# A residual stream kept in expert order: token rows scattered once, no padding, output rows scattered at the end

## The chip, the cores and the metric

The kernel runs on one core of a Trainium2 chip. The metric is the device time of one execution in microseconds (us). A core has TensorE (PE, matrix products), VectorE (DVE), ScalarE (ACT), GpSimd (POOL) and SyncE (SP), each with its own instruction stream. They order themselves by semaphores. SyncE and GpSimd issue DMA transfers; indirect ones (a row address per partition, from a table) come from GpSimd.

## The reference

One decoder layer on x of 4 x 512 tokens with 512 features (2048 tokens, 16 tiles of 128 rows):

```python
x = x + attn(_layernorm(x))                          # linear attention, 16 heads of 32
x = x + experts(_layernorm(x), itok, ctx, ctx, ctx)  # expert of a token: from its token id
x = x + ffn(_layernorm(x))                           # ternary weights, 512 -> 2048 -> 512

# attn:    q = elu(x Wqk + bqk) by heads, v = silu(x Wv + bv), u = silu(x Wu + bu)
#          out = q (k^T v) per head; out = layernorm(out) * ln_g + ln_b
#          return (u * out) @ Wo + bo
# experts: e = min(token_id // 6250, 3); g = silu(x ctx[e]^T); u = x ctx[e]^T
#          return (g * u) @ ctx[e]^T           (512 x 512 per expert, 4 experts)
# ffn:     w -> clip(round(w / scale), -1, 1) * scale, scale = mean(|w|)
#          return (silu(x wu^T) * (x wg^T)) @ wd^T
```

The drawn token ids spread over the four experts, so the number of tokens of an expert is not a multiple of 128.

## The kernel before

[...] 

**Attention**, four batches of four tiles. `batch(b, first, last)` exists on each engine. PE makes q (four products of 12 matmuls), v, the output projection of the batch before (`project`), key transposes, u (four products), the key-value sums (L1230) and the head products (L1244). The head norm and the projection of batch b - 1 are done inside batch b, and those of the last batch behind the loop: filler matmuls (`keep_busy`), `head_norm`, `project`, then VectorE's `last_sum` and `last_norm`. A normalised tile (n2) is scattered by GpSimd (`scatter`, L328) into the DRAM tensor `sorted_tokens`, at row positions in which each expert begins at a multiple of 128; before, ten SyncE stores fill this tensor with zeros, for the padding rows. Positions are made on VectorE in `routing_starts` and `routing_positions`, at the end of the first batch.

**Experts**, 19 tiles (16 + 3 for padding; `SLOTS`). For a tile: SyncE loads it (`sorted_tile`), PE transposes it (`xs_transpose`), ACT and DVE make a high and a low half in float16 (`xsT`), PE makes z, ACT and DVE make z * silu(z) (h_mul), PE transposes that, and `second(i - 1)` is the product of the tile before. The weights are picked by a register that PE reads (`tile_expert`). VectorE copies the result (`y_copy`), GpSimd stores it to `sorted_outputs`.

**Ternary units.** The three weight matrices of the last stage come in 12 units of 1 MB. VectorE makes two sign passes (`signs_of`), PE transposes them (`unit_transposes`, 32 matmuls), ACT copies (`unit_copies`). Before, four units are ahead of the expert tiles (the fourth behind the first transpose), five in steps 0 to 3, three behind the last tile, followed by 96 filler matmuls.

**Last stage.** Four batches, 16 chunks each of two 8-matmul groups (up, gate; L1350) and eight down matmuls (L1360). For its first batch, GpSimd gathers four tiles from `sorted_outputs` back into token order, VectorE sums, makes statistics and norms, PE transposes and ACT and DVE split. For later batches one tile is gathered, summed and normalised every four chunks, and turned by a DMA transpose (`x3_turned`). `finish` adds the residual, and SyncE stores the output tiles (`stored`).

## Time and profile before

| | before |
|---|---|
| median of 3 runs | 757.99 us (757.53 to 758.48) |
| profiled execution, its own time | 756.31 us |
| its span | 754.7 us |
| PE busy | 726.2 us, 96% |
| VectorE, ScalarE, GpSimd busy | 388.9, 275.9, 108.6 us |
| mean granted clock of PE | 0.989 of full speed |
| memory traffic | 47.73 MB read, 18.61 MB written |

The span is the time from the first to the last record of the profile; the own time is what a timer around the execution shows. PE's busy time counts overlapping instructions once. [...] Positions in a row are us from the start of the span.

### The profile page before, as it was taken

How to read it: one execution, taken by the hardware profiler on the slowest of the kernel's cores; microseconds unless marked ns; L12 is line 12 of the kernel's file. 1: busy time of each engine (PE TensorE's matmuls, PEld its weight loads, DVE VectorE, ACT ScalarE, POOL GpSimd, SP SyncE). 2: the span in 40 equal slices, each digit the busy share in tenths (PEclk: the TensorE clock that was granted, in tenths of full speed). 3: DMA queues.
4: the chain of work that ended last, by engine and by line, in shares of the span. 5: the costliest groups of instructions: out<-in, count | busy, mean ns of one | idle time of the engine just before them, and what ended most of it. 6: DMA issues, size and time to landing. Idle time of an engine off the chain costs nothing.

```text
span 754.7 us, 12300 instructions
## 1 busy us (share of the span) xinstructions
PE 726.2 (96%) x4136; PEld 391.0 (52%) x4137; DVE 388.9 (52%) x672; ACT 275.9 (37%) x430; POOL 108.6 (14%) x154
## 2 busy tenths in 40 slices
PE   7999999999997889999997999999999999999997
PEld 5565556556556666555546444444444444444443
DVE  5678666666636955444457433454434534443223
ACT  4365554554554355222324222222223222222221
POOL 4203034034021400000004100000000000000000
PEclk9999999999999999999999899999999999999999
DMA  8983034034044396222212011121101210020001
GB/s 238 391 322 137 1 128 151 0 127 152 1 159 176 113 361 231 79 85 96 83 42 71 28 29 28 28 80 33 24 19 28 83 28 14 14 70 0 0 0 57
DMA packets 45168, 69.93 MB, mean 93 GB/s; under 512 B 19024, under 2 KB 19024, under 8 KB 44112
## 3 DMA queue, kind: packets, MB, share of 16 engines
q1 hardware_dynamic: 41136, 56.38, 22.4%
q0 software_dynamic: 4000, 13.11, 5.0%
q8 instruction: 21, 0.34, 0.2%
q14 instruction: 11, 0.09, 0.0%
HBM read 47.73 MB, written 18.61 MB: 88 GB/s over the span
## 4 chain that ended last, share of the span: by engine, by line
PE 85%; DVE 4%; DMA 3%; issue 2%; ACT 2%; POOL 2%; SPq 1%; DVEq 0%; POOLq 0%; ACTq 0%
PE bank L1079 31%; PE bank L1350 30%; PE bank L1360 14%; PE bank L1072 5%; PE bank L1230 2%; PE bank L1244 1%; DMA nrm<-in_L_ffn_W_down_dram 1%; PE bank L1265 1%; DMA stage<-in_L_attn_Wv_dram 1%; POOL rs L320 1%; DVE st L589 1%; DMA sorted_tokens<-n,pos_now 1%; SPq L184 1%; DMA n<-sorted_outputs,pos_now 0%; DVE region L774 0%
## 5 line engine op out<-in xcount | busy, mean ns | idle before, releaser
L1350 PE MATMUL bank<-w_att,region 128*128 128x512 f16 (+1 forms) x1024 | 233.4, 381 | 0.8 <-ACT w_att L550 0.8
L1350 PEld LDWEIGHTS bank<-w_att,region 128*128 (+1 forms) x1024 | 100.6, 98 | 123.3 <-issue 3.9
L1045 DVE SCALAR_TENSOR_TENSOR tmp<-tmp,hk,bank 128x512 f32<-128x512 f32 x64 | 47.8, 747 | 150.2 <-PE bank L1350 149.8
L1360 PE MATMUL bank<-region,tmpA 128*128 (+1 forms) x504 | 119.1, 379 | 0.0
L1079 PE MATMUL bank<-w_moe,tmpA 128*128 x456 | 104.9, 380 | 1.5 <-DVE tmpA L934 1.5
L1079 PE MATMUL bank<-xT,w_att 128*128 128x512 f16 x384 | 86.6, 381 | 1.6 <-DVE region L774 1.6
L564 ACT ACTIVATE tmp<-bank,qs 128x512 f32<-128x512 f32 x64 | 44.0, 687 | 119.5 <-PE bank L1350 119.5
L568 ACT ACTIVATE tmpA<-tmp 128x512 f16<-128x512 f32 x64 | 40.3, 630 | 122.0 <-DVE tmp L1045 122.0
L1360 PEld LDWEIGHTS bank<-region,tmpA 128*128 128x128 f16 x504 | 49.2, 98 | 59.6 <-DVE stage L1028 0.9
L1079 PEld LDWEIGHTS bank<-w_moe,tmpA 128*128 128x128 f16 x456 | 44.5, 98 | 47.2 <-issue 2.0
L1048 DVE TENSOR_TENSOR tmpA<-tmp,tmpA 128x512 f16<-128x512 f32 x64 | 44.3, 693 | 45.6 <-ACT tmpA L568 45.6
L318 POOL TENSOR_SCALAR ve<-mv 128x1 f32<-128x1 f32 (+1 forms) x37 | 10.2, 275 | 381.1 <-DVE mv L1008 204.6
L1079 PEld LDWEIGHTS bank<-xT,w_att 128*128 128x128 f16 x384 | 37.3, 98 | 44.4 <-DVE region L774 2.4
L1079 PE MATMUL bank<-w_att,region 128*128 128x512 f16 x192 | 43.0, 383 | 1.0 <-DVE region L727 1.0
L1079 PE MATMUL bank<-w_att,xT 128*128 128x512 f16 x192 | 42.8, 379 | 0.0
L501 ACT ACTIVATE region<-bank 128x512 bf16<-128x512 f32 x48 | 25.3, 603 | 28.9 <-PE bank L1265 24.7
L1079 PEld LDWEIGHTS bank<-w_att,region 128*128 128x128 f16 x192 | 18.6, 98 | 24.2 <-DVE region L727 2.2
L1079 PEld LDWEIGHTS bank<-w_att,xT 128*128 128x128 f16 x192 | 18.7, 98 | 21.3 <-DVE region L731 0.5
L1265 PE MATMUL bank<-ident_b,w_att 128*128 128x128 bf16 x384 | 24.9, 226 | 4.0 <-DVE w_att L864 4.0
L929 DVE TENSOR_TENSOR tmp<-bank,tmp 128x512 f32<-128x512 f32 x19 | 13.1, 690 | 28.7 <-ACT tmp L529 28.7
L1265 PEld LDWEIGHTS bank<-ident_b,w_att 128*128 128x128 bf16 x384 | 23.4, 102 | 6.1 <-DVE w_att L864 4.9
L320 POOL TENSOR_TENSOR rs<-ve,halfs 128x1 f32<-128x1 f32 (+1 forms) x37 | 25.8, 698 | 3.1
(138 smaller groups left out, 769.9 us busy)
## 6 DMA issues: line engine op xcount, KB each, us to landing
stage<-in_L_ffn_W_up_dram SPq DMA_DIRECT2D x8, 1024.0 KB
stage<-in_L_ffn_W_gate_dram SPq DMA_DIRECT2D x8, 1024.0 KB, 5.6
sorted_tokens<-a SPq DMA_DIRECT2D x10, 512.0 KB, 10.7
n<-sorted_tokens SPq DMA_DIRECT2D x20, 256.0 KB, 2.6
stage<-in_ctx_dram SPq DMA_DIRECT2D x4, 1024.0 KB
stage<-in_L_ffn_W_down_dram SPq DMA_DIRECT2D x4, 1024.0 KB
nrm<-in_L_ffn_W_down_dram SPq DMA_DIRECT2D x4, 1024.0 KB, 7.7
out_dram<-stage SPq DMA_DIRECT2D x16, 256.0 KB, 2.1
```

Source lines behind the costliest of these rows:

```text
L320: pool.tensor_tensor(rs[i][:, tiles], ve[i][:, tiles], halfs[:, tiles], ALU.pow).then_inc(s[done], 1)
L501: act.activation(dst, src, ACT.Copy).then_inc(s["unit_copy"], 1)
L564: act.activation(sil, up_ps[:, :], ACT.Silu, scale=qs[:, 0:1]).then_inc(s["up_act"], 1)
L568: act.activation(hid[:, cc % 2, 0], h32, ACT.Copy).then_inc(s["hid_hi"], 1)
L1045: dve.scalar_tensor_tensor(out=h32, in0=sil, scalar=hk[:, 0:1], in1=gate_ps[:, :], op0=ALU.mult, op1=ALU.mult).then_inc(s["hid_mul"], 1)
L1048: dve.tensor_tensor(hid[:, cc % 2, 1], h32, hid[:, cc % 2, 0], ALU.subtract).then_inc(s["hid_lo"], 1)
L1072: mm = pe.transpose(dst[:, i * P:(i + 1) * P], src(i), ident[:, :])
L1079: mm = pe.matmul(dst, lhs(*step), rhs(*step), start=(start and n == 0), stop=(stop and n == len(steps) - 1))
L1230: mm = pe.matmul(kv_ps[:, cut], kk[:, t, cut], vv[:, t, cut], start=(t == 0), stop=(t == T - 1))
L1265: mm = pe.matmul(q_ps[r][:, cut], signs[:, j, h, r, cut], ident_b[:, :], start=(h == 0), stop=(h == 1))
L1350: mm = pe.matmul(dst, w[:, bass.ds(cf_c, 1), k * P:(k + 1) * P].rearrange("p a n -> p (a n)"), x3T[:, bass.ds(b, 1), i, k].rearrange("p a ...
L1360: mm = pe.matmul(ffy_ps[t][:, :], hid[:, parity, i, t * P:(t + 1) * P], tern[2][:, bass.ds(c, 1)].rearrange("p a n -> p (a n)"), start=(st ...
```

## The change

The tokens stay in expert order from the scatter to the output.

- Positions have no padding: expert e begins where e - 1 ends. A tile of 128 sorted rows can hold rows of several experts. 19 steps (`STEPS`) walk through pairs of tile and expert: step i works on tile i - expert, and `routing_steps` makes the tables of expert, tile, address of the tile, and for each step a column `own` that is 1/65536 for rows of the step's expert and 0 for others. VectorE adds y * own into the residual tile (`y_add`, tile by register). No zeros are stored.
- The residual tiles are scattered as well, into `sorted_residual`, by GpSimd (16 transfers), and loaded back in this order by SyncE (four of 1 MB); so are the row numbers, into `sorted_ids` (16 transfers of 128 x 4 bytes), and read back as `row_id`.
- The sorted tiles are transposed once and their halves stay in the buffer of the attention weights (`sorted_T`, the same memory as `x3T`), from which PE's first product reads at a register address. Sign buffers move to `late`, two in place of three, over buffers of the attention stage.
- Ten units stand in steps 0 to 9; none behind the last step. Filler: 70 matmuls behind the first unit; the 50 and the 96 are gone.
- The first four tiles of the last stage are normalised in steps 13 to 18 and turned by DMA; there is no gather. Outputs are scattered by GpSimd to their token rows.
- In the last attention batch the four u products come behind the head products, in the place of the filler.
- Loops over batches (GpSimd) and steps (all engines) are written out.

The diff, cut:

```diff
@@ sync
-                sp.wait_ge(s["zero_src"], 1)
-                with sp.Fori(0, (SLOTS + 1) // 2) as i:
-                    sp.dma_start(xs_v[:, bass.ds(2 * i, 2)], a32[:, :, :]).then_inc(s["zeroed"], 16)
...
+        sp.wait_ge(s["scattered"], 16 * NT)
+        for i in range(3):
+            sorted_tile(i)
         sp.wait_ge(s["sign_b"], 1)
         unit(1, 0)
...
+        sp.wait_ge(s["x1_sent"], 16 * NT)
+        sorted_residual(0)
+        sp.wait_ge(s["sign_b"], 2)
+        unit(1, 1)
+        sp.wait_ge(s["sign_b"], 3)
+        unit(1, 2)
+        for n in range(6):
+            sp.wait_ge(s["tx_mm"], n + 1)
+            sorted_tile(n + 3)
+            if n % 2 == 0:
+                sorted_residual(1 + n // 2)
+            sp.wait_ge(s["sign_b"], n + 4)
+            unit(2 + n // 3, n % 3)
@@ gpsimd
+        def scatter_residual(b):
+            for n in range(T * b, T * b + T):
+                pool.indirect_dma_start(x1_dram, row_of(n), resid[:, n], None).then_inc(s["x1_sent"], 16)
+
+        def scatter_ids(b):
+            for n in range(T * b, T * b + T):
+                pool.indirect_dma_start(id_dram, row_of(n), tok_id[:, n:n + 1], None).then_inc(s["id_sent"], 16)
...
+            if 0 < b < B - 1:
+                scatter_residual(b - 1)
+                scatter_ids(b - 1)
...
         for t in range(T):
             rsqrt_tile(1, "o_aggr", T * (B - 1), t, "rs_o_last")
+        scatter_residual(B - 2)
+        scatter_ids(B - 2)
+        scatter_ids(B - 1)
         rsqrt_tile(2, "x2_aggr", T * (B - 1), 0, "rs2_last")
...
         scatter(B - 1, T - 1)
+        pool.memset(halfs[:, :], -0.5).then_inc(s["scatter_out"], 1)
+        scatter_residual(B - 1)
+        def send_out(b):
+            for t in range(T):
+                pool.wait_ge(s["out_made"], T * b + t + 1)
+                pool.indirect_dma_start(out_rows, bass.IndirectOffsetOnAxis(ap=row_id[:, T * b + t:T * b + t + 1], axis=0),
+                                        out_slot[t], None).then_inc(s[f"out_done{t}"], 16)
@@ scalar
+        ctx_hi(B - 1, 3)
+        magnitudes(B - 1, 0)
+        act.wait_ge(s["a_mul"], K * (B - 1))
+        o_copies(B - 1)
+        magnitudes(B - 1, 1)
+        u_act(B - 1, 0)
+        magnitudes(B - 1, 2)
+        u_act(B - 1, 1)
+        u_act(B - 1, 2)
         affine(B - 1, 0)
+        affine(B - 1, 1)
+        gated_hi(B - 1, 0)
+        gated_hi(B - 1, 1)
+        u_act(B - 1, 3)
@@ vector, routing_steps at the end of the first batch (count_of: three comparisons, two sums)
+            count_of(expert, at, [pad_f[:, 1, e:e + 1] for e in range(1, E)])
+            route(dve.scalar_tensor_tensor(out=tile, in0=expert, scalar=-float(P), in1=at, op0=ALU.mult, op1=ALU.add))
+            route(dve.tensor_scalar(row, tile, lane[:, 0:1], None, ALU.add))
+            count_of(of_row, row, [base[:, e:e + 1] for e in range(1, E)])
+            route(dve.tensor_tensor(own[:, :], of_row, expert, ALU.is_equal))
+            route(dve.tensor_scalar(own[:, :], own[:, :], CTX_SCALE ** -2, None, ALU.mult))
@@ vector, the steps
+        dve.wait_ge(s["scatter_out"], 1)
         signs_of(0, 1)
...
-            dve.tensor_scalar(ys_slot[slot], y_ps[:, :], CTX_SCALE ** -2, None, ALU.mult).then_inc(s["y_evac"], 1)
+            dve.scalar_tensor_tensor(out=x_tile(tile), in0=y_ps[:, :], scalar=own[:, i:i + 1], in1=x_tile(tile),
+                                     op0=ALU.mult, op1=ALU.add).then_inc(s["y_evac"], 1)
...
+        def expert_step(i):
+            if i == 0:
+                signs_of(0, 2)
+            elif i < 10:
+                signs_of(1 + (i - 1) // 3, (i - 1) % 3)
             dve.wait_ge(s["z_act"], i + 1)
             dve.wait_ge(s["h_hi"], i)
             dve.tensor_tensor(h32, z_ps[:, :], sil, ALU.mult).then_inc(s["h_mul"], 1)
+            if i + 1 < NT:
+                xs_lo(i + 1)
+            if 15 <= i:
+                x3_lo(i - 15)
+            if i > 0:
+                y_add(i - 1)
+            if 14 <= i < 14 + T:
+                x3_normalise(i - 14)
             dve.wait_ge(s["h_hi"], i + 1)
             dve.tensor_tensor(hT[:, 1], th_ps[:, :], hT[:, 0], ALU.subtract).then_inc(s["h_lo"], 1)
+            if 13 <= i < 13 + T:
+                if i == 13:
+                    dve.wait_ge(s["y_evac"], i)
+                x3_stats(i - 13)
@@ tensor
-        keep_busy(kv_ps, 50)
+        u_part(B - 1, 0, False)
+        u_part(B - 1, 1, False)
+        u_part(B - 1, 2, False)
+        head_norm(B - 1, True, (0, 1))
+        u_part(B - 1, 3, False)
+        head_norm(B - 1, True, (2, 3))
...
+        def first(i):
+            w = weights_of(i)
+            off = pe.value_load(step_off[0:1, i:i + 1], min_val=0, max_val=(B - 1) * 2 * K * S + S - P)
+            pe.wait_ge(s["xs_lo"], min(i, NT - 1) + 1)
+            pe.wait_ge(s["h_mul"], i)
+            product(z_ps[:, :], lambda i, j, k: sorted_T[:, bass.ds(off + (i * K + k) * S, P)], w).then_inc(s["z_mm"], 1)
...
-        keep_busy(ps[3], 96)
...
         pe.wait_ge(s["unit_copy"], 12 * T)
+        pe.wait_ge(s["y_evac"], STEPS)
+        pe.wait_ge(s["x3_in"], 16 * T)
```

How the change moves instructions, at three places. In these rows a name is an engine's tile: bank is a PSUM bank, region holds q, k, v, u and the gated rows, late the transposed inputs and later the signs, ones the filler's operand.

On PE, behind the last batch's key transposes, there stood before:

```order
L1079 MATMUL bank<-xT,w_att 128x512 x12
L1072 MATMUL bank<-ident,stage 128x128 x4
L1079 MATMUL bank<-xT,w_att 128x512 x36
L1230 MATMUL bank<-region 128x128 x16
L1244 MATMUL bank<-kvm,region 128x128 x16
L1086 MATMUL bank<-ones 128x128 x50
L1282 MATMUL bank<-abssum,ones 128x3
L1072 MATMUL bank<-ident,region 128x128 x16
L1079 MATMUL bank<-w_att,region 128x512 x48
```

and now:

```order
L1063 MATMUL bank<-ident,stage 128x128 x4
L1227 MATMUL bank<-region 128x128 x16
L1241 MATMUL bank<-late,region 128x128 x16
L1070 MATMUL bank<-late,w_att 128x512 x36
L1063 MATMUL bank<-ident,region 128x128 x8
L1070 MATMUL bank<-late,w_att 128x512 x12
L1063 MATMUL bank<-ident,region 128x128 x8
L1285 MATMUL bank<-abssum,ones 128x3
L1070 MATMUL bank<-w_att,region 128x512 x48
```

The four u products (48 matmuls) moved from ahead of the key-value sums to behind the head products, around the head transposes.

On GpSimd, from the last four rsqrts of the head norm to the last scatter, now (before, the two rows with sorted_residual and sorted_ids were not there):

```order
L309 TENSOR_SCALAR ve<-mv 128x1
L311 TENSOR_TENSOR rs<-ve,halfs 128x1
L326 DMA sorted_residual<-resid,pos 2048x512 x4
L330 DMA sorted_ids<-tok_id,pos 2048x1 x8
L309 TENSOR_SCALAR ve<-mv 128x1
L311 TENSOR_TENSOR rs<-ve,halfs 128x1
L309 TENSOR_SCALAR ve<-mv 128x1
L311 TENSOR_TENSOR rs<-ve,halfs 128x1
L322 DMA sorted_tokens<-n,pos 2048x512
```

Twelve indirect transfers moved in between the last head rsqrt and the first rsqrt of the last normalisation.

On PE, from the last expert product to the last stage, before:

```order
L1079 MATMUL bank<-w_moe,tmpA 128x512
L1265 MATMUL bank<-ident_b,w_att 128x128 x96
L1086 MATMUL bank<-ones 128x128 x96
L1072 MATMUL bank<-ident,nrm 128x128 x16
L1350 MATMUL bank<-w_att,region 128x512 x32
```

and now:

```order
L1070 MATMUL bank<-w_moe,tmpA 128x512 x2
L1070 ISA
L1070 MATMUL bank<-w_moe,tmpA 128x512
L1342 MATMUL bank<-w_att,region 128x512 x32
L1352 MATMUL bank<-region,tmpA 128x512 x8
```

Three units, the filler and the four transposes of the first normalised tiles are gone from between them.

## Rows read from the trace of the kernel before

**Rows 1.** The page: busy time and share, and PE in 40 slices.

```profile
PE 726.2 (96%) x4136; PEld 391.0 (52%) x4137; DVE 388.9 (52%) x672; ACT 275.9 (37%) x430; POOL 108.6 (14%) x154
...
PE   7999999999997889999997999999999999999997
```

**Rows 2.** Table by stages: stage, length, PE, PEld, DVE, ACT, POOL busy, clock, DMA.

```profile
225.00:270.00 45.00, 36.88 (x359) 28.36 (x358) 30.97 (x56) 18.39 (x32) 12.97 (x20) 0.93 0.48 176
...
396.00:416.00 20.00, 14.85 (x210) 12.74 (x207) 15.00 (x26) 8.71 (x16) 10.29 (x13) 0.94 0.21 67
```

**Rows 3.** Chain that ended last: start, length, what.

```profile
258.69 4.68 DMA sorted_tokens<-n,pos_now
...
397.00 2.03 DMA sorted_outputs<-n
...
416.06 9.16 PE bank L1350 x32
426.94 3.45 PE bank L1350 x16
```

**Rows 4.** PE's instructions in order: start, length, instruction, count.

```profile
285.33 2.75 PE L1079 MATMUL bank<-w_moe,tmpA 128*128 x12
...
293.18 2.75 PE L1079 MATMUL bank<-w_moe,tmpA 128*128 x12
...
388.36 0.60 PE L1072 MATMUL bank<-ident,n 128*128 128x128 f32 x4
388.80 2.75 PE L1079 MATMUL bank<-w_moe,tmpA 128*128 x12
391.39 0.60 PE L1072 MATMUL bank<-ident,tmp 128*128 128x128 f32 x4
393.49 2.76 PE L1079 MATMUL bank<-w_moe,tmpA 128*128 x12 [1.50 <-DVE tmpA L934]
```

**Rows 5.** PE's instructions, end of attention and start of experts.

```profile
228.85 3.96 PE L1244 MATMUL bank<-kvm,region 128*128 128x128 f32 x32 [0.78 <-DVE kvm L836]
...
244.13 9.38 PE L1079 MATMUL bank<-w_att,region 128*128 128x512 f16 x42 [0.51 <-DVE region L727]
...
269.70 2.98 PE L1079 MATMUL bank<-w_moe,tmpA 128*128 x12
```

**Rows 6.** VectorE's instructions, end of attention.

```profile
236.82 0.55 DVE L597 TENSOR_SCALAR region<-region,mv,rs 128x512 f32<-128x512 f32 x1 [0.76 <-POOL rs L320]
...
247.17 0.68 DVE L750 TENSOR_TENSOR resid<-bank,resid 128x512 f32<-128x512 f32 x1
...
256.52 0.55 DVE L597 TENSOR_SCALAR n<-resid,mv,rs 128x512 f32<-128x512 f32 x1 [0.77 <-POOL rs L320]
```

**Rows 7.** GpSimd's instructions, end of attention.

```profile
223.98 0.96 POOL L328 DMA_INDIRECT sorted_tokens<-n,pos_now  x1 [0.30 <-issue]
...
258.69 2.09 POOL L328 DMA_INDIRECT sorted_tokens<-n,pos_now  x1 [0.30 <-issue]
```

**Rows 8.** The line that reads a tile's expert, 330 to 343 us.

```profile
L1299 PEldq TENSOR_LOAD <-tile_expert x4: 297/300/307, 331.6 to 341.7; - x4
```

**Rows 9.** VectorE's instructions, end of the first batch.

```profile
61.94 0.16 DVE L684 CAST starts<-starts_i 1x19 f32<-1x19 int32 x1
...
63.08 0.16 DVE L691 CAST tile_expert<-te_f 1x19 int32<-1x19 f32 x1
...
68.55 0.70 DVE L772 TENSOR_SCALAR tmp<-tmp 128x512 f32<-128x512 f32 x1 [2.34 <-ACT tmp L441]
```

**Rows 10.** Last issues (start, length), then DMA issues with median us to landing.

```profile
750.11 2.31 SPq L277 DMA_DIRECT2D out_dram<-stage  x4
...
n<-sorted_tokens SPq DMA_DIRECT2D x20, 256.0 KB, 2.6
...
out_dram<-stage SPq DMA_DIRECT2D x16, 256.0 KB, 2.1
...
n<-sorted_outputs,pos_now POOLq DMA_INDIRECT x16, 3.4
```

More of the change, by code:

```diff
@@ L469, in batch @@
                 ctx_hi(b, 0)
+            if last:
+                return
             magnitudes(b, 0)
@@ L824, in batch @@
                 ctx_lo(b, 3)
+                if last:
+                    kv_mask(b)
                 dve.wait_ge(s["rs2"], 2 * b)
@@ L1308, in second @@
             pe.wait_ge(s["y_evac"], i)
-            moe(y_ps[:, :], hT, e).then_inc(s["y_mm"], 1)
-        def tile_step(i, units, slot, slot_count, first):
-            e = expert(i)
-            pe.wait_ge(s["xs_lo"], i + 1)
-            pe.wait_ge(s["h_mul"], i)
-            moe(z_ps[:, :], xsT, e).then_inc(s["z_mm"], 1)
-            xs_transpose(i + 1, slot, slot_count)
-            if not first:
+            product(y_ps[:, :], lambda i, j, k: hT[:, i, k * P:(k + 1) * P], w).then_inc(s["y_mm"], 1)
@@ L1318, in tile_step, with expert_step @@
+        def expert_step(i):
+            first(i)
+            if i + 1 < NT:
+                xs_transpose(i + 1)
+            if i > 0:
                 second(i - 1)
-            for g, j in units:
-                unit_transposes(g, j)
+            if i == 0:
+                unit_transposes(0, 2)
+            elif i < 10:
+                unit_transposes(1 + (i - 1) // 3, (i - 1) % 3)
             pe.wait_ge(s["h_mul"], i + 1)
```

552 lines of the change are left out of this document (239 added, 313 removed).

## The prediction

> **What bounds the kernel now.** I read the page first: TensorE (PE) is busy 96% of the span [rows 1], so time goes away only where PE works without use or waits. Its row of 40 slices is full but for the first and last one, slices 13 to 15 and slice 22, and the table by stages shows two holes: 225 to 270 us holds only 36.9 us of PE work, and 396 to 416 us only 14.9 us [rows 2]. Both counts include matmuls that only keep PE busy. The chain that ended last says what these two places wait for [rows 3]. Before the experts it is the scatter of the last normalised rows, which lands 4.68 us after 258.69. After the experts it is a round trip through memory: a 2.03 us store of the last expert outputs at 397.00, then a gather, sums, statistics, norms and transposes until the last stage starts at 416.06. [...]
>
> The instruction list of PE gives the pace between the two. The first product of one step with a sign unit starts at 285.33, the next one's at 293.18: 7.85 us. A step without a unit is two products of 12 matmuls (2.59 us each, from 388.80 to 391.39) and two groups of transposes (0.44 us each, 388.36 to 388.80), 6.06 us [rows 4]. So a unit costs 7.85 - 6.06 = 1.79 us of PE, and there is no bubble in either kind of step.
>
> **The end of the attention stage.** Before, PE goes through the head products at 228.85, then 50 filler matmuls and the head transposes, and has 42 projection matmuls left at 244.13, which end at 253.5 [rows 5]. Afterwards the four u products (4 x 2.59 = 10.4 us) stand behind the head products and fill what the filler and the waits took. Head products can start about 9.9 us earlier, at 219 (10.4, less some 0.5 for key copies that the u products used to cover); they take 3.9 us. Three u products run to 230.7. The last head norm ended at 237.37 [rows 6], some 8.5 us behind the start of the head products; now four norms of the third batch (1.9 us) and its four scatters are ahead of it on VectorE and GpSimd, so I take 11 us: 230. It is met by PE at 230.7. The rest (transposes, u product 3, transposes: 4.4 us) ends at 235.1. The gating of the last two chunks follows, 3.5 us (half of the 6.8 us between 237.37 and 244.13), and 38 matmuls remain at 216 ns, 8.2 us: the projection ends at 247, not 253.5.
>
> VectorE carries the chain on. Its last norm ended at 257.07, 9.9 us after the first residual sum at 247.17 [rows 6]. From 242 (gating, scales, one pair of sign passes) it would end at 251 to 252. But GpSimd now has 12 indirect transfers (four of residual rows, eight of ids) in its queue ahead of the last rsqrts. One takes 0.96 us and a gap of 0.30 [rows 7], so 12 take 15.1 us; with the start at 229 and a sign pair (2.5 us) in their way, the first rsqrt can start at 247, where it is wanted at 243.7. This takes back about 2.5 us: last norm at 254, last two scatters done at 256, landed at 259, instead of 263.4. The first sorted tile is read next (2.6 us, [rows 10]), turned on PE (0.44 us) and split by ScalarE and VectorE (0.6 and 0.7 us, the times of such passes elsewhere), so the first expert product starts 4.5 us later, at 263.5, instead of 269.70 [rows 5], since the three units that stood before it are now inside the steps or done already. Id transfers are not in the trace. Their bounds are nothing (below) and 2.09 us each (above, the slowest scatter [rows 7]); I take the residual's price, as both have 128 rows. The bounds are then 243.7, no delay, or a first rsqrt at 256, 9 us late.
>
> The slowest scatter started at 258.69, under a pair of sign passes: 2.09 us, against 0.96 [rows 7]. The wait that the change adds ahead of the next sign passes spares the last scatters this, about 1.9 us together, contained in the sum. [...]
>
> **The staircase.** 19 steps before and after, 38 products. Transposes of sorted tiles fall from 19 to 15 in the steps; ten units instead of five stand in them. PE work: 38 x 2.59 + 34 x 0.44 + 10 x 1.79 = 131.3 us, plus the 1.5 us wait ahead of the last product [rows 4]; plus 1.7 us because PE will be nearly idle before it, as it was before the 9.16 us row, where the low clock cost 2.26 us (bounds 0 and 2.3). From 263.5 the last product ends at 398.0. The last stage now waits for the last VectorE sum, 0.75 us: 398.8.
>
> Three things could lengthen steps, and I cost each at nothing. The register work: the reads of the step's expert take 0.30 us each [rows 8], PE's sequencer does them ahead of the array, and now two stand before the first product with four more register instructions. In steps without units they must fit between the end of h_mul (about 1.4 us after a product: a silu and a multiplication of 0.6 to 0.7 us) and 3.03 us; two reads with what follows take 1.0 us. If the cover were gone: 0.5 us x 9 plain steps. VectorE: the sum replaces a copy of the same 0.69 us, norms, statistics and low halves of the first four tiles are four passes more in a 5.6 us step that had four such passes of 0.6 to 0.7 us. DMA: the second and third unit loads stand behind the last residual scatter (landed at about 263) and a 1 MB load; both land by 272, wanted at 280. Turning the first batch by DMA: the last of the four is issued behind step 18's first product, 7 us before PE is through; if it takes what a gather takes, 3.4 us [rows 10], more than 2 us are left. Its upper bound is 2 us past that.
>
> **The last stage** thus starts at 398.8 against 416.06: -17.3. Its slow first matmuls: PE idles only 1.5 and 0.8 us before it now, so I take the 2.26 us as gained: -2.3 (bounds 0 and -2.3). Inside it, a sum, a gather and a position copy per tile go, all hidden under PE; nothing.
>
> **Early cost.** The tables of steps, tiles and lanes are made at the end of the first batch on VectorE. The old tail of seven instructions takes from 61.94 to 63.24 [rows 9], 0.19 us each; 33 take 6.1 us: +4.8 us. Statistics of the heads queue behind it, then the q clip of the next batch, which had waited 2.34 us for ScalarE [rows 9]; PE waits for it. So +2.4 us, all batches later. Residual scatters of batches 0 and 1 on GpSimd (8 transfers, 10.1 us each time) stand behind the last rsqrt that a batch of 56 us waits for, on an engine that is busy 14% of the time [rows 1]: nothing; if they did delay the next rsqrt, 10 us at most. The 10 zeroing stores go, nothing waited for them; nothing.
>
> **The end.** Output tiles leave by SyncE, issue to landing 2.1 us; the last four issues begin at 750.11 and end at 752.42 [rows 10]. Now GpSimd scatters them: four at 1.26 us, so the last is issued at about 754.0 and lands 3.4 us later (the gathers' median [rows 10]): 757.4 against 754.2, +3.2. A scatter may land as the fastest gather would, 2.5 us: +2.3.
>
> **Sum**: -17.3 - 2.3 + 2.4 + 3.2 = -14.0 us against the profiled execution, whose own time is 756.31 with a span of 754.7; so 742.3, and with the median of the runs (757.99, 1.7 above it) 744.0.
>
> **Rivals.**
> (a) GpSimd's queue is late, in the form in which it still ends faster: the twelve transfers cost the upper bound, the experts start 6 us later than I say. 750.0. [...]
> (b) Other side: the same queue decides alone if the twelve take so long that the first rsqrt starts 14 us later than 247, that is (261 - 229)/12 = 2.7 us each. At 3.0 us each it starts at 265, 18 us late, and the time is 762.0, slower. Against it: no transfer in the trace takes that long; for it: ids of 4 bytes are in no row.
> (c) The steps become issue-bound: every matmul of the first product needs two registers. If it took 260 ns, not 216, a step grows by 0.53 us, 10 us in all: 754.0. Against it: the reads of 0.30 us and eight register instructions per product leave no bubble in the steps before [rows 4, 8], so the sequencer is well ahead of the array.
> (d) Nothing is lost on GpSimd: ids are cheap and the clock stays up: 740.0.
> (e) The change doesn't do what it says: the last stage still waits for the turned first tiles. They have 2 us or more to spare; each tile late by more adds that. 747.0 for 3 us more.
>
> **How the numbers follow.** Forecast and its surroundings (741 to 748) 0.52, (d) 0.13, (a) 0.12, (e) 0.08, (c) 0.07, (b) 0.08. Range 738 to 752: it leaves out (b), (c) and the far ends, under 2 in 10. The measurement can tell some 0.2% (1.5 us). Faster needs under 756.5: all but (b) and the worst of (c): 0.90; same 0.03; slower 0.07.
>
> **What would show it.** PE's gap before the last stage under 3 us with no filler; head products near 221 (with the early cost) and experts' first product near 266; steps of 7.85 and 6.06, then 5.6 us; VectorE's tables some 6 us at 62; final landing some 7 us behind the last matmul. It would be wrong if GpSimd's transfers before the last rsqrt took over 25 us together, if steps with units grew past 7.9 us, or if the batches' PE work gained new waits.

## The result, and the profile after

The change makes the kernel slower. In the same session of the chip the kernel after took 765.56 us (median of 4 runs, 763.66 to 766.73) and the kernel before 757.76 us (4 runs, 757.15 to 758.48). The ratio is 1.010, with a 95% interval of 1.0077 to 1.0123. The prediction was 744.0 us, 738 to 752. The profiled execution of the kernel after, the fastest of the four, has an own time of 763.66 us and a span of 761.9 us.

The page of the kernel after: busy time and share, and PE in 40 slices.

```profile
PE 715.7 (94%) x3948; PEld 381.1 (50%) x3978; DVE 386.8 (51%) x655; ACT 273.1 (36%) x426; POOL 131.0 (17%) x171
...
PE   8998999899899869999998999999999999999993
```

PE has 10.5 us less work than in [rows 1] and the span is 7.2 us longer. Slice 22, after the experts, reads 8 instead of 7; the attention batches (slices 4 to 11) now have three slices of 8 where all were full, slice 15 (the switch to the experts) has 6, and in the last slice PE works 3 tenths instead of 7.

The table by stages, of the kernel after, with the columns of [rows 2].

```profile
225.00:270.00 45.00, 39.85 (x308) 26.88 (x305) 29.32 (x62) 21.19 (x32) 29.86 (x37) 1.00 0.49 176
270.00:396.00 126.00, 118.40 (x857) 72.78 (x858) 71.02 (x92) 49.38 (x93) 7.97 (x10) 0.99 0.46 157
396.00:416.00 20.00, 18.50 (x92) 8.99 (x90) 10.97 (x19) 5.45 (x9) 1.57 (x4) 1.00 0.24 46
```

The stage from 396 to 416 us holds 18.50 us of PE work where it held 14.85 [rows 2]: this hole is mended. The stage from 225 to 270 us holds more too (39.85 instead of 36.88), but everything here comes some five us later than before, and a part of the hole now lies behind 270: PE waits there for 5.5 us until 273.78, and the row from 270 to 396 us holds 118.40 us (124.16 before). The chain that ended last shows where the time went instead (start, length, what).

```profile
138.50 5.65 DVE late L759
...
146.19 7.04 PE bank L1070 x24
...
200.07 5.74 DVE late L759
...
207.84 7.04 PE bank L1070 x24
...
417.43 7.07 PE bank L1342 x32
```

One VectorE multiplication (L759, the gating product `gated_mul`) takes 5.65 us in the third batch and 5.74 us in the last one, and PE's next 24 matmuls take 7.04 us where 24 take 5.26 us elsewhere: PE had waited for 3.24 us, and the mean granted clock (the share of PE's full speed that the profile shows) behind the wait is 0.65 for 2.4 us and 0.80 for the next 4.4, a mixture of 0.50, which the trace has from 146.93 to 150.35 us, and 1.00 on both sides of it. The last stage starts at 417.43 instead of 416.06 [rows 3]; its first 32 matmuls take 7.07 us instead of 9.16.

VectorE's instructions (start, length, line, operation) and under them GpSimd's, both in the third batch of the kernel after.

```profile
137.90 0.68 DVE L799 SCALAR_TENSOR_TENSOR w_moe<-bank,w_moe 128x512 f32 x1
138.50 6.24 DVE L759 TENSOR_TENSOR late<-tmpA,region 128x512 f32<-128x512 f32 x2
144.84 0.69 DVE L763 TENSOR_TENSOR region<-late,region 128x512 f16<-128x512 f32 x1
...
128.42 1.08 POOL L326 DMA_INDIRECT sorted_residual<-resid,pos  x1 [0.19 <-issue]
...
137.68 0.96 POOL L330 DMA_INDIRECT sorted_ids<-tok_id,pos  x1 [0.30 <-issue]
138.66 4.92 POOL L335 TENSOR_TENSOR resid<-resid,bo_bc 128x512 f32<-128x512 f32 x4
```

GpSimd's eight transfers fill 128.42 to 138.64, and the four bias adds that used to follow the rsqrt (the reciprocal square root of a norm) at once now start at 138.66, 0.16 us behind the gating product. VectorE's first multiplication then ends only when the four bias adds end (at 144.15 us, they at 143.58). The one reads `tmpA` and `region`, the other `resid` and `bo_bc`.

PE's instructions around it, and at the last product and the last stage.

```profile
140.19 2.75 PE L1070 MATMUL bank<-w_att,late 128*128 128x512 f16 x12
146.19 7.04 PE L1070 MATMUL bank<-w_att,late 128*128 128x512 f16 x24 [3.24 <-DVE region L767]
...
413.67 2.76 PE L1070 MATMUL bank<-w_moe,tmpA 128*128 x12 [1.50 <-DVE tmpA L1002]
417.43 7.07 PE L1342 MATMUL bank<-w_att,region 128*128 128x512 f16 x32 [1.00 <-issue]
```

The end of the program, in GpSimd's instructions, and then the DRAIN instructions that the engines' queues have at the end of the block, of the kernel after (lengths in ns, start us).

```profile
749.63 0.96 POOL L374 DMA_INDIRECT out_dram<-stage,row_id  x1 [73.43 <-DVE stage L1020]
...
753.42 0.96 POOL L374 DMA_INDIRECT out_dram<-stage,row_id  x1 [0.30 <-issue]
...
L1399 DVEq DRAIN  x1: 2218/2218/2218, 749.2 to 749.2; - x1
...
L1399 POOLq DRAIN  x1: 5292/5292/5292, 756.4 to 756.4; - x1
```

The last scatter has landed at 756.4. What follows is not a transfer: it is GpSimd's own closing DRAIN, 5.29 us, to 761.7. In the kernel before the same instruction stood at 647.3, a hundred us ahead of the end:

```profile
L1408 POOLq DRAIN  x1: 4661/4661/4661, 647.3 to 647.3; - x1
```

### The profile page after: what moved, and what is told of

Its sections match the earlier page's. It is cut to its first block, busy times and chain, and to the rows that moved or that the text cites. A ratio compares the mean times of both kernels' runs of the same rounds, so it can differ in the third digit from the quotient of the medians.

```text
span 761.9 us, 11591 instructions
## 1 busy us (share of the span) xinstructions
PE 715.7 (94%) x3948; PEld 381.1 (50%) x3978; DVE 386.8 (51%) x655; ACT 273.1 (36%) x426; POOL 131.0 (17%) x171
## 4 chain that ended last, share of the span: by engine, by line
PE 82%; DVE 6%; POOL 4%; issue 3%; ACT 2%; SPq 1%; DMA 1%; DVEq 0%; ACTq 0%; POOLq 0%
PE bank L1342 29%; PE bank L1070 28%; PE bank L1352 14%; PE bank L1063 4%; PE bank L1263 3%; PE bank L1227 2%; DVE late L759 1%; POOL sorted_ids L330 1%; PE bank L1241 1%; POOL sorted_tokens L322 1%; DMA stage<-in_L_attn_Wv_dram 1%; DVE region L606 1%; POOL sorted_residual L326 1%; SPq L190 1%; DVE st L598 1%
## 5 line engine op out<-in xcount | busy, mean ns | idle before, releaser
L1070 PE MATMUL bank<-late,w_att 128*128 128x512 f16 x384 | 86.1, 379 | 4.0 <-DVE region L806 3.9
L1070 PEld LDWEIGHTS bank<-late,w_att 128*128 128x128 f16 x384 | 37.2, 98 | 46.4 <-DVE region L806 4.7
L1070 PE MATMUL bank<-w_moe,w_att 128*128 x228 | 52.4, 380 | 3.8 <-issue 2.2
L1070 PE MATMUL bank<-w_moe,tmpA 128*128 x228 | 52.3, 379 | 1.5 <-DVE tmpA L1002 1.5
L1070 PE MATMUL bank<-w_att,late 128*128 128x512 f16 x192 | 46.5, 400 | 6.6 <-DVE region L767 6.6
L1070 PEld LDWEIGHTS bank<-w_moe,w_att 128*128 x228 | 22.2, 97 | 28.3 <-issue 6.8
L374 POOL DMA_INDIRECT out_dram<-stage,row_id x16 | 16.2, 1012 | 110.4 <-DVE stage L1020 108.0
L1070 PEld LDWEIGHTS bank<-w_att,late 128*128 128x128 f16 x192 | 19.2, 102 | 31.3 <-DVE region L767 8.1
L1070 PEld LDWEIGHTS bank<-w_moe,tmpA 128*128 128x128 f16 x228 | 22.2, 98 | 25.3 <-issue 2.0
L1263 PE MATMUL bank<-ident_b,late 128*128 128x128 bf16 x384 | 24.8, 225 | 5.5 <-DVE late L903 5.5
```

The lines of the kernel that those rows point to most:

```text
L374: pool.indirect_dma_start(out_rows, bass.IndirectOffsetOnAxis(ap=row_id[:, T * b + t:T * b + t + 1], axis=0), out_slot[t], None).then_inc( ...
L1070: mm = pe.matmul(dst, lhs(*step), rhs(*step), start=(start and n == 0), stop=(stop and n == len(steps) - 1))
L1263: mm = pe.matmul(q_ps[r][:, cut], signs[:, u % 2, h, r, cut], ident_b[:, :], start=(h == 0), stop=(h == 1))
```

## The experiments

Seventeen kernels ran. Ratios are to the kernel before in the same session; its medians there lay between 755.8 and 757.8 us.

**1. The bias adds back in their place.** The changed kernel, with the eight transfers behind the next batch's bias adds instead of ahead of them.

```diff
 def batch(b):
     ... (bias adds of batch b)
+    if b > 1:
+        scatter_residual(b - 2)
+        scatter_ids(b - 2)
     ...
-    if 0 < b < B - 1:
-        scatter_residual(b - 1)
-        scatter_ids(b - 1)
```

> The changed kernel with one thing moved: GpSimd's eight transfers of residual rows and ids of a batch stand behind the four bias adds of the next batch, not ahead of them. Theory A (the bias adds, which read two tiles, now run at the time of VectorE's gating product, which reads two tiles as well, and hold it for 5 us in each of two batches): the 5.65 us gating product returns to 0.7 us, PE's two waits of 3.2 and 3.3 us go, some 10 us less: 755 to 756. Rival (the indirect transfers themselves hold VectorE or the memory): they now run just at the time of the gating product, it stays long, the time stays near 765.

Measured: 757.45 us (10 runs), ratio 1.001 (0.9994 to 1.0026). One edit in GpSimd's order gives back 8.1 us by the medians, 7.1 if each is taken against the kernel before of its own session. VectorE's and GpSimd's rows of this run:

```profile
138.87 1.28 DVE L759 TENSOR_TENSOR late<-tmpA,region 128x512 f32<-128x512 f32 x2
...
128.58 5.55 POOL L335 TENSOR_TENSOR resid<-resid,bo_bc 128x512 f32<-128x512 f32 x4
134.30 1.48 POOL L326 DMA_INDIRECT sorted_residual<-resid,pos  x1 [0.17 <-issue]
```

The two gating products take 1.28 us again instead of 6.24, beside transfers instead of bias adds.

**2. The same collision in the kernel before.** The kernel before, with eight spare transfers at the place where the changed kernel has its own.

```diff
 rsqrt(1, "o_aggr", T * b + T, slice(0, T), "rs_o", b)
+if not first and not last:
+    for n in range(8 * b - 8, 8 * b):
+        pool.indirect_dma_start(more_dram, bass.IndirectOffsetOnAxis(ap=pos[:, n:n + 1], axis=0),
+                                ones[:, :], None).then_inc(s["more_sent"], 16)
 ...
-with pool.Fori(1, B - 1) as b:
+for b in range(1, B - 1):
     batch(b, False, False)
```

The loop over the two middle batches is written out as well, on GpSimd, as it is in the kernel after.

> The kernel before, with eight indirect transfers of 128 rows to a spare DRAM tensor behind the head's rsqrt in each of the two middle batches, at the place where the changed kernel has its residual and id transfers; nothing else of the change. Theory A: the bias adds behind them are delayed by 10 us onto the gating product, which costs 5 us in each of two batches: 768. Rival (the long batches come from something else in the change, the address of the transposed inputs or the written-out loops): 758, no change.

Measured: 767.23 us, ratio 1.0135 (1.0102 to 1.0169): the whole loss and more, without a residual stream that is sorted. The written-out loop alone was not run; the rows show the transfers' part. Here it is another VectorE instruction that is caught, a copy of 4 integers per partition:

```profile
136.43 5.10 DVE L767 COPY pos_now<-pos 128x4 int32 x1
...
136.57 4.92 POOL L336 TENSOR_TENSOR resid<-resid,bo_bc 128x512 f32<-128x512 f32 x4
```

**3. Register reads earlier.** In the changed kernel, the two reads of the next step's expert and offset are made ahead of the unit's 64 weight loads and matmuls, not behind them.

```diff
-def expert_step(i):
-    first(i)
+def expert_step(i, reads):
+    first(i, *reads)
     ...
+    reads = reads_of(i + 1) if i + 1 < STEPS else None
     (unit transposes, then those of h)
+    return reads
```

> The changed kernel with PE's two register reads for the next step's first product placed ahead of the unit transposes, not behind the h transposes. Theory B (in steps with a unit PE's sequencer is no further ahead than the last few matmuls, so the two reads of 0.30 us each with their register work show as the 0.8 us, not 0.44 us, from h transposes to product): unit steps fall from 8.22 to 7.85 us, ten of them, some 3.5 us less: 762. Rival (first products are slow to start because both operands have register addresses): steps stay at 8.22 us, 765.6.

Measured: 761.79 us, ratio 1.0078 (1.0052 to 1.0104): 3.8 us less by the medians, 2.8 against the kernels before of the two sessions; ten steps by 0.37 us make 3.7. PE's rows, first of the kernel after, then of this run:

```profile
300.57 0.61 PE L1063 MATMUL bank<-ident,tmp 128*128 128x128 f32 x4
301.38 2.76 PE L1070 MATMUL bank<-w_moe,w_att 128*128 x12 [0.20 <-issue]
...
309.58 2.76 PE L1070 MATMUL bank<-w_moe,w_att 128*128 x12 [0.19 <-issue]
```

```profile
300.95 0.61 PE L1063 MATMUL bank<-ident,tmp 128*128 128x128 f32 x4
301.40 2.75 PE L1070 MATMUL bank<-w_moe,w_att 128*128 x12
...
309.24 2.75 PE L1070 MATMUL bank<-w_moe,w_att 128*128 x12
```

From the transposes to the product it takes 0.81 us in the one and 0.45 us in the other, from step to step 8.20 and 7.84 us. The gap of 0.37 us is shown as only 0.20 "issue", since the recorded end of the transposes lies 0.16 us behind the start of the next product where nothing is waited for.

**4 and 5. The end of the program.** In run 4 the last four output tiles are stored by SyncE in sorted order, so this kernel leaves out the way back to the token rows for them, and its output is not the reference's; the amount of work is the same. In run 5 the scatters stay, but SyncE waits for their landing instead of GpSimd.

```diff
 send_out(B - 1)
-for t in range(T):
-    pool.wait_ge(s[f"out_done{t}"], 16 * B)
 (SyncE, at its end)
+for t in range(T):
+    sp.wait_ge(s[f"out_done{t}"], 16 * B)
```

> The changed kernel with the last four output tiles stored by SyncE as they lie (the rows of these tiles stay in expert order in the output), so that GpSimd's last transfer is 70 us before the end. Theory C (GpSimd's drain at the end of the program takes 5.3 us, and starts only when its last transfer has landed; before it lay under PE): 7.3 us less, 758.3. Rival (only the transfers are slower, 2.7 against 2.1 us and 1.26 against 0.66 us apart): 2.5 us less, 763.

> The changed kernel, with one edit: SyncE instead of GpSimd waits for the last output scatters to land, so GpSimd's program ends with its last issue (754.38) instead of with the landing (about 756.1), and its final DRAIN can begin some 2 us earlier. Theory: the DRAIN is a fixed piece of some 5.3 us behind GpSimd's last instruction, so the span ends near 759.7 instead of 761.7 and the median is 763.5. Rival: the DRAIN itself waits for the transfers, in which case it begins earlier and is as much longer, and the median stays at 765.5. A DRAIN that costs nothing once its transfers are waited for elsewhere would give 760.

Measured: run 4 757.72 us, ratio 1.002 (1.0003 to 1.0037), 7.8 us less than the kernel after (6.9 by the sessions). Run 5 764.35 us, ratio 1.0089 (1.0063 to 1.0115), too near to 1.010 to tell by time; its trace tells it. The last scatter is over at 757.14 and SyncE knows of its landing at 759.2; GpSimd's DRAIN (recorded from 754.1, 8312 ns) ends at 762.4, 5.3 us behind its last instruction, as it ended 5.3 us behind the wait in the kernel after:

```profile
756.18 0.96 POOL L376 DMA_INDIRECT out_dram<-stage,row_id  x1 [0.30 <-issue]
...
L1399 POOLq DRAIN  x1: 8312/8312/8312, 754.1 to 754.1; - x1
...
L1399 SPq DRAIN  x1: 13/13/13, 759.2 to 759.2; - x1
```

So it is a piece of 5.3 us behind whatever GpSimd does last, in both kernels. From the last scatter's end to the span's end it is now 5.6 us, and was 7.5 (754.38 to 761.9).

**6. Ids later.** The eight id transfers ahead of the last norm moved behind the last residual scatter.

> The changed kernel, with one edit: the eight id transfers of batches 2 and 3 go behind the last residual scatter instead of ahead of the first reciprocal square root of the last norm. The twelve transfers took 244.41 to 261.72, so four take some 5.7 us and end near 250, before the square root is wanted at 258.2. Theory (the queue of twelve costs 2 us or a little more): VectorE's wait of 2.76 at 262.68 shrinks to the 0.8 that the square root takes, the staircase starts 2.0 earlier, median 763.5. Rival (what the front gains is lost again behind it, because the wait for the sorted rows or the clock decides): 765.5.

Measured: 777.62 us, ratio 1.0265 (1.0233 to 1.0298): 12 us worse than the kernel after. The near part came as expected (the pair of sign passes that waits for the scatters starts at 269.31 instead of 271.24), the rest did not. Three loads of 1 MB took 20.7 to 23.7 us to land, where the same three took 9.9 to 13.3 in the kernel after, and PE waited once for 8.04 us:

```profile
308.60 1.12 PE L1063 MATMUL bank<-ident,n 128*128 128x128 f32 x4 [8.04 <-DMA n<-sorted_tokens]
```

**7. Tables later.** The tables of tile, offset and expert made behind the second pair of sign passes, where VectorE idles some 5 us.

> The changed kernel, with one edit: the 28 or so small VectorE operations that make the tables of tile, offset and expert (62.81 to 68.40, 5.6 us) are moved from the end of the first batch to the place behind the second sign pass pair, where VectorE idles 5.4 us for the first sorted tile. Theory (they cost some 2.3 us where they stand: a TensorE wait of 2.38 instead of 0.63 at 72.83 and 0.86 at 79.05): the second batch's products start 2.3 earlier and the median is 763.2. Rival (the time at the front is given back later through the clock, or the new place is on the path to the first expert product): 765.5 to 766.

Measured: 764.96 us, ratio 1.0113 (1.0084 to 1.0142). The key-value sums of the first two batches are 58.97 us apart, not 61.15, and the next two 59.95, not 61.65, but the first product of the experts waits 3.12 us for the tables and runs 5.16 us, at a granted clock of 0.50. VectorE had made the tables by 275.56 us, and only then the low half of the first tile. The rival was right: nothing clear of noise is left at the end.

**8. All of them.** Edits 1, 3, 5, 6 and 7 together.

> The changed kernel with the edits of the bias-add run, the early register reads, the late ids, the late tables and SyncE's final waits together. Theory (the costs are separate and add): 757.5 from the bias-add run, less 3.8 of the register reads, less 2.0 of the ids, less 2.3 of the tables, less 1 to 2 of the end if the DRAIN is a fixed piece: 748, between 746 and 750, faster than the kernel before (756.8) by 1.1 per cent. Rival (the gains overlap, since a shorter middle lets TensorE's clock fall more often or the last stage waits for another engine): 752 or more.

Measured: 761.3 us, ratio 1.0052 (1.0031 to 1.0074). The theory failed by 13 us; the late ids are in it.

**9 to 12. Ids in the second batch.** Positions are known after the first batch, so all sixteen id transfers can be issued in the second one, where GpSimd idles for 30 us. Run 9 does this on top of run 1. Run 10 adds eight spare scatters of 2 KB rows behind the last residual scatter, where run 6 had its ids. Runs 12 and 11 add edits 3 and 5, with the tables early and late.

```diff
 (GpSimd, behind the bias adds of batch b)
+if b == 1:
+    pool.wait_ge(s["rows_made"], 1)
+    for n in range(B):
+        scatter_ids(n)
 if b > 1:
     scatter_residual(b - 2)
```

> The kernel with the bias-add run (757.45), with one more edit: all sixteen id transfers are issued in the second batch, behind GpSimd's bias adds, where GpSimd idles from 78.7 to 108.8 (16 by 1.27 is 20.3 us); none is left in the middle batches or ahead of the last norm. Theory (ids cost only where they stand in the way or run beside the weight loads): the 2.76 us wait for the first reciprocal square root of the last norm falls to 0.8, and nothing is lost elsewhere: 755.4. Rival (an id transfer slows the DMA engines wherever it stands, or the gain is lost at the switch to the experts): 757.5 or more.

> The kernel with early ids, plus eight spare scatters of 2 KB rows (to a tensor that nothing reads) behind the last residual scatters, where the run with late ids had its eight transfers of 4-byte rows. GpSimd's time for them is the same 10 us. Theory (it was the 4-byte rows that slowed the DMA engines there: a 6 us stretch moved 13 GB/s and loads landed in 17 to 24 us instead of 8 to 10): the spare rows add 2 MB, some 5 us of the DMA engines' time, most of it hidden: within 3 us of the kernel with early ids, 755.4 to 758.5. Rival (any eight scatters there hold up the loads or the instruction fetches behind them): 12 us more, 767.

> Bias adds first (757.45), ids early (less 2.0), register reads early (less 3.8), GpSimd's program ending with its last issue (less 2.0), the tables at their first place: 749.7 if the four add, between 748 and 752, faster than the kernel before by 0.9 per cent. Rival (a gain is lost again at the switch to the experts, through the clock or late instructions): 754 or more.

> Bias adds first, ids early, register reads early, GpSimd's program ending with its last issue, and the tables of tile and expert made behind the second sign pass. Theory (the tables' early cost of some 2 us is saved and the new place hides them): 1 to 2 us below the same kernel with the tables at their first place, 748. Rival (the new place puts the first expert product behind the tables' 5.6 us, so what is gained at the front is lost there): 750 or more, the same as or slower than the kernel with the tables at their first place.

Measured: run 9 760.11 us (ratio 1.0044), 2.3 to 2.7 slower than run 1; run 10 766.14 (1.0129), 6 slower than run 9: near the rival's time, but with half of the 12 us that it named (four of its five times lie at 765.6 to 766.7, the profiled one at 760.6, so its trace does not show this loss); run 12 753.02 (0.9952), run 11 753.86 (0.9952). The last two beat the kernel before by 0.5%, but all four are slower than expected. In run 9 the second batch is 8.4 us longer, with one wait of VectorE:

```profile
98.74 0.95 POOL L330 DMA_INDIRECT sorted_ids<-tok_id,pos  x1 [0.30 <-issue]
...
92.14 0.69 DVE L769 TENSOR_TENSOR region<-bank,bv_bc 128x512 f32<-128x512 f32 x1 [2.10 <-PE bank L1072]
100.62 0.69 DVE L769 TENSOR_TENSOR region<-bank,bv_bc 128x512 f32<-128x512 f32 x1 [7.79 <-remote]
```

The wait marked "remote" ended with a semaphore update recorded at 100.60 us; the product of PE that it tells of had ended at 92.01. I first read it as a late fetch of instructions: from 88 to 92 us the profile has one packet of 0.01 MB in the instruction queue q14, and it took 6.0% of the time of the 16 DMA engines in this run, 0.5% in run 1.

**13 to 15. Which property of the transfers.** Run 13 is run 12 with the ids in the third batch, whose code has run once already; run 14 the same of run 11; run 15 is run 13 with sixteen scatters of 2 KB rows in the second batch.

> The kernel with bias adds first, early register reads, GpSimd's early end and the tables at their first place (753.0 with the ids in the second batch), with the sixteen id transfers moved from the second batch to the third, behind the residual scatters. Theory (an id transfer costs by holding up instruction packets; the third batch runs the loop's body a second time and fetches nothing): no VectorE wait of several us, the second batch is back to the 61.4 between the key-value sums that the kernel without ids there had (71.3 now in the profiled run), and the median is 747 to 749.5. Rival (4-byte rows slow whatever runs beside them): the loss moves to the third batch with them, 753.

> The same as the run with the ids in the third batch, with the tables of tile and expert made behind the second sign pass (753.9 with the ids in the second batch). Theory (the tables' cost at the front is 2.3, but most of it is lost again, since the first expert product then waits for the tables): within 1.5 us of the run with the tables at their first place, 748. Rival (the place decides): 2 to 3 us below it, 745.5.

> The run with the ids in the third batch, plus sixteen spare scatters of 2 KB rows in the second batch, where the ids had cost several us. Theory (only 4-byte rows hold up the instruction packets there): an instruction packet in the second batch stays near the 0.3 to 1.2 us it had without ids, no VectorE wait of several us, and the time is within 1 us of the run with the ids in the third batch. Rival (any sixteen scatters there cost it): 4 to 5 us more.

Measured: 763.27, 760.78 and 773.89 us (ratios 1.0092, 1.0064, 1.0221). The fetch theory falls: there is no instruction packet between 132 and 178 us of run 13, and the loss is there, larger, since twenty transfers now stand in a row (four residual ones are ahead of the ids): 71.4 us between the key-value sums, where run 12 had 56.5. The theory of small rows falls too: in run 15, 2 KB rows cost 10.6 us. VectorE's rows of run 13:

```profile
146.39 0.69 DVE L769 TENSOR_TENSOR region<-bank,bv_bc 128x512 f32<-128x512 f32 x1 [3.39 <-PE bank L1072]
...
153.52 0.69 DVE L769 TENSOR_TENSOR region<-bank,bv_bc 128x512 f32<-128x512 f32 x1 [4.45 <-remote]
163.45 0.69 DVE L769 TENSOR_TENSOR region<-bank,bv_bc 128x512 f32<-128x512 f32 x1 [9.24 <-remote]
```

VectorE waits there for products of PE. The trace has the ends of these products and the recorded updates of the semaphore that tells of them (us; the ends of matmuls are modelled):

```
                              product 1          product 2          product 3
run 1, second batch, idle     86.77 ->  86.78    89.36 ->  89.37    91.94 ->  91.96
run 1, third batch            143.31 -> 146.15   145.90 -> 146.27   149.69 -> 149.70
run 13, third batch           143.57 -> 146.37   146.16 -> 153.49   149.90 -> 163.42
run 15, second batch, 2 KB    87.22 ->  87.23    89.81 ->  92.53    92.40 ->  98.24
transfers: run 1 from 134.30 to 144.83 (8), run 13 from 134.56 to 160.47 (20),
           run 15 from 79.61 to 100.10 (16)
```

Without transfers the update comes 0.01 us behind the product. Some nine or ten us into a run of transfers it is 2.7 to 2.8 us late, and if the run goes on, 5.8, 7.3 and 13.5 us; if the run ends, the updates are on time again. Run 15's third batch, with twenty transfers again, repeats run 13 (2.8, 7.4 and 13.5 us). Run 9's wait of 7.79 us is the same thing: the product ends at 92.01, the update comes at 100.60.

**16 and 17. The length of the run.** The same sixteen ids, eight in the second batch and four behind each four residual scatters, so that no run in the batches is longer than eight and four stand ahead of the last norm; with the tables early (16) and late (17).

```diff
 if b == 1:
     pool.wait_ge(s["rows_made"], 1)
-    for n in range(B):
-        scatter_ids(n)
+    scatter_ids(0)
+    scatter_ids(1)
 if b > 1:
     scatter_residual(b - 2)
+    scatter_ids(b)
```

> Bias adds first, early register reads, GpSimd's early end, tables at their first place, and the sixteen ids spread: eight in the second batch, four behind each four residual scatters in the third and fourth. Theory (only a run of transfers longer than some ten delays TensorE's semaphores; eight in a row cost next to nothing, as in the first run): no wait of VectorE for a late update, key-value sums 61 to 62 apart in the second batch and 57 in the third, and the median is 757.4 less 3.8, 2.0 and 2.0: 749.6, between 748 and 751. Rival (each transfer costs about 0.6 us wherever it stands beside matmuls): 753 or more, as in the run with all ids in the second batch.

> The same with the tables of tile and expert made behind the second sign pass. With the tables late the ids cost some 3 us less in the profiled second batch, and the first expert product waited 4.7 us for the tables. Theory (gain at the front 2.3, most of it given back at the switch): 748.5 to 750, the same as or up to 1 us below the kernel with the tables at their first place. Rival (the place of the tables decides 2 us or more): below 747.5.

Measured: 747.58 us (5 runs, 745.94 to 750.1), ratio 0.9878 (0.9856 to 0.9901), and 747.43 us (4 runs), ratio 0.9874 (0.9856 to 0.9893). The same number of transfers as in run 12, 5.4 us faster. The third batch lost time with a long run in it (run 13) and loses next to none with a run of eight, so it is the length of the run that decides and not the batch. Runs of eight are not free of it: in run 16 the latest update in a batch comes 2.1 us behind its product (142.78 to 144.88). Both are 1.2% faster than the kernel before. In run 16's table by stages PE is busy for all 126 us of the experts (118.40 in the kernel after):

```profile
225.00:270.00 45.00, 36.23 (x281) 22.36 (x280) 27.93 (x52) 18.91 (x29) 24.82 (x33) 0.97 0.61 213
270.00:396.00 126.00, 126.00 (x886) 75.38 (x885) 74.26 (x102) 51.08 (x96) 3.15 (x8) 1.00 0.41 135
```

## Why the prediction was wrong

The sum gave 742.3 against the profiled execution, whose own time is 763.66: 21.4 us too little. By its own steps:

**The step that failed** is "Residual scatters of batches 0 and 1 on GpSimd … nothing". It asked whether the next rsqrt would be late, and it was not. It did not ask who stands behind the transfers on GpSimd: four bias adds, pushed 10 us on, onto VectorE's gating product. Between the key-value sums of the second and third, and of the third and fourth batch, there are 61.65 and 51.26 us; before there were 56.54 and 55.60, and the latter now holds 10.4 less work. That is 5.1 and 6.1 us lost, 11 together. PE's rows of the key-value sums, of the kernel before, then of the kernel after:

```profile
112.19 3.74 PE L1230 MATMUL bank<-region 128*128 128x128 f32 x32
...
168.73 3.74 PE L1230 MATMUL bank<-region 128*128 128x128 f32 x32
...
224.33 3.73 PE L1230 MATMUL bank<-region 128*128 128x128 f32 x32
```

```profile
116.21 3.74 PE L1227 MATMUL bank<-region 128*128 128x128 f32 x32
...
177.86 3.74 PE L1227 MATMUL bank<-region 128*128 128x128 f32 x32
...
229.12 3.74 PE L1227 MATMUL bank<-region 128*128 128x128 f32 x32
```

In run 1 they are 57.74 and 46.08 us, 9.1 less, and run 2 makes the loss in the kernel before; this is shown, not argued. By what way the one instruction holds up the other is not shown. In the rows VectorE got no turn between the four bias adds (5.65 us against 1.23 us for one add). In the two meetings in the kernel after and the two in run 2 the record of VectorE's instruction starts first, by 0.14 to 0.23 us, and it is VectorE that is held. The copy of run 2 reads one tile only and is held as well (5.10 us), so two inputs are not needed for it. I had weighed only the other direction, a GpSimd transfer that takes longer under VectorE's sign passes (2.09 us against 0.96 [rows 7]).

**The end** was priced +3.2. The landing was no worse than priced (3.0 us from the last scatter's start, 3.4 allowed), the DRAIN was missing: from PE's last matmul to the span's end it is 4.8 us before (749.84 to 754.68) and 12.8 now (749.12 to 761.93), +8.0. I had read the last issues and landings, not what the queues do after them. Run 4 gives back 7.8 (6.9 by the sessions), and in run 5 the DRAIN again ends 5.3 us behind GpSimd's last instruction.

**Register reads** were among the three things of which the prediction said "I cost each at nothing", with 0.5 us for each of 9 plain steps as the price if it was wrong. The nine plain steps indeed showed nothing (6.05, then 5.7); the ten steps with a unit took 8.2 us, past the 7.9 that it had named as a sign, and lost 0.37 us each. There the reads stand behind 64 weight loads and matmuls in PE's queue, with only the four transposes of h (0.44 us) between them and the product that needs two reads of 0.30 us; run 3, which moves them ahead, gives back 3.8 us.

**The start** came 1.0 us late (key-value sums of the first batch at 55.06 instead of 54.07). The tables took 5.6 us and PE's waits behind them grew by 2.6 (2.38 and 0.86 us instead of 0.63) where I had +2.4. The second of these waits is the bias adds again: four norms of the heads (L606) take 5.11 us beside them, and 2.08 in run 7, where the adds (68.59 to 73.90) had all but ended when the norms began (73.47). Why the first key-value sums are already 1.0 us late is not known. Runs 16 and 17 show that moving the tables gains nothing at the end.

**Right**: from the head products to the experts' first product 45.5 us (233.64 to 279.11), forecast 44.5; VectorE waited 2.76 us for the first rsqrt behind the twelve transfers, forecast 2.5 to 3.3 (the slowest of them took 2.42 us, under a pair of sign passes from 254.07 to 256.55); the projection ended 28.9 us behind the head products, forecast 28; the slow first matmuls, -2.1 us instead of -2.3 (before, 9.16 us less twice 3.45 [rows 3] is 2.26, and the trace has a granted clock of 0.50 from 413.50 to 420.33); the last stage itself, 324.6 us in both from the end of its first 32 matmuls to PE's last.

From the first expert product to the last stage it is 138.3 us, forecast 135.3. The forecast held 1.7 us for a low clock at its start. It fell on the 32 sign transposes ahead of the first product (3.31 us instead of 1.95, with a granted clock of 0.50 from 273.23 to 276.64 us) and is in the 45.5 us above; the product itself took 2.76 us, at a granted clock of 1.00. So this stretch is 4.7 us over, 3.7 of it the reads, and that it looks only 3 us off is luck.

So the expected gain was there and was given back: 12.2 us by the head products (11 of them in those two batches), 1 in the tail, 3 net in the steps, 4.8 at the end, 21 together. None of the rivals named the place; (b), slower through the twelve transfers, gave about the right time (762.0) for a wrong reason. Rival (c) had all steps too long by 0.53 us each; ten of them were, by 0.37.

What stays open: by what way a long run of indirect transfers delays TensorE's semaphore updates. Twelve in a row ahead of the last norm (244.41 to 261.72) delayed none that the trace shows (updates 0.02 us behind the products), though they took longer than those that did; neither the size of the rows (run 15) nor instruction fetches (run 13) explain it. Nor is it settled how much of run 6's and run 10's loss is this and how much the slower loads.

## What to carry to other kernels

When work is put into a queue "that is idle most of the time", look at what stands behind it there, when that will now run, and beside what: bias adds of 4.92 us that were hidden become 5 us of the path when they meet an instruction of another engine that they hold up (1.28 us for two gating products in run 1, 6.24 in the kernel after). Price the end of a program with the engine that ends last, its closing DRAIN included (here 5.29 us of GpSimd), and let GpSimd finish early: from its last scatter's end to the span's end it was 7.5 us where it waited for the landing and 5.6 where SyncE did. And split long runs of indirect transfers; here the same sixteen cost 5.4 us more in one piece than in pieces of eight and four, and 15.7 us more in one piece with four others ahead of them (run 13 against run 16).

## What the hardware showed that was not expected

- GpSimd's closing DRAIN took 5.29 us behind its last wait in the kernel after (4.66 us in the kernel before), VectorE's 2.2, ScalarE's 0.5, SyncE's 0.4 or less.
- A transfer of 128 rows of 4 bytes took GpSimd 0.96 us, four times in the third batch of the kernel after; one of 128 rows of 2 KB took 0.97 to 1.23.
- A semaphore update of TensorE was recorded up to 13.5 us behind its product, in a run of 20 transfers (runs 13 and 15).
- A copy of 4 integers per partition was held for 5.10 us by four bias adds of another engine (run 2).
